# Expert weights copied and split in place, sixteen tile buffers, and the routed tiles of the last groups issued behind the shared part

## What is computed

```python
x = x + attn(layernorm(x), Wq, Wk, Wv, Wr)                  # self-attention, 16 heads of 64, causal
x = x + xattn(layernorm(x), ctx, ctx, w_q, w_k, w_v, w_o)   # cross-attention, 16 heads
x = x + ffn(layernorm(x), ...)

# ffn, flat = the 2048 tokens
shared = swiglu(flat @ w_in.T) @ w_out.T
g_probs = softmax(flat @ wg.T + gb)            # 2 groups
g_idx = argmax(g_probs)
masked = where(g_idx == group of expert, flat @ we.T + eb, -inf)
p_expert = softmax(masked) * g_probs[g_idx]    # 8 experts, 4 a group
topv, topi = top_k(p_expert, 2)                # always two experts of the chosen group
h = swiglu(flat @ w1.T)                        # 512 wide, the same for every expert
routed = sum over the two experts: (h * weight) @ w2[e].T
out = x + shared + routed
```

## Time and profile before

| | us |
|---|---|
| median of the three runs | 945.33 |
| the profiled execution | 941.11 |
| span of the profile, first to last instruction | 939.3 |
| attention, to the barrier | 0 to 649.6 |
| feed-forward, to the first slot scatter | 649.6 to 726.3 |
| scatters and what PE does beside them, to the first `turn` | 726.3 to 790.4 |
| 39 expert tiles | 790.4 to 870.3 |
| last shared units, gathers, output | 870.3 to 939.3 |

### The profile page before, as it was taken

One profiled execution on the slowest core, in us unless ns is written; L12 is line 12 of the kernel. 1 busy time (PEld: TensorE's weight loads), 2 busy tenths in 40 slices (PEclk: granted clock), 3 DMA queues, 4 the chain that ended last, 5 costly groups with the idle time before them and its releaser, 6 DMA issues. The chain is left out here.

```text
span 939.3 us, 17987 instructions
## 1 busy us (share of the span) xinstructions
PE 851.3 (91%) x6115; PEld 741.0 (79%) x6115; DVE 596.2 (63%) x1513; ACT 546.3 (58%) x1667; POOL 304.0 (32%) x318
## 2 busy tenths in 40 slices
PE   8999999999999989999999999998787748999841
PEld 6788888888888878988988898896575637999731
DVE  5787787687778767667767766775768214333153
ACT  4877677677668776866677686775343113554110
POOL 1443124124123434421432341351333750000544
PEclk9999999999999999999999999999897969999976
DMA  7680000000001020000000020010120532664233
GB/s 240 245 312 2 1 0 0 0 0 0 0 1 46 24 68 1 1 23 1 0 22 0 0 80 9 1 46 1 67 68 23 206 152 95 205 199 149 79 90 112
DMA packets 34105, 60.35 MB, mean 64 GB/s; under 512 B 3460, under 2 KB 15108, under 8 KB 34052
## 3 DMA queue, kind: packets, MB, share of 16 engines
q1 hardware_dynamic: 29956, 47.07, 15.0%
q0 software_dynamic: 4096, 12.59, 4.0%
HBM read 33.83 MB, written 25.82 MB: 64 GB/s over the span
## 5 line engine op out<-in xcount | busy, mean ns | idle before, releaser
L420 POOL TENSOR_TENSOR prob<-prob,rsum 128x512 f32<-128x512 f32 x128 | 133.4, 1042 | 395.0 <-DVE rsum L613 395.0
L498 ACT ACTIVATE prob<-psS,nmin 128x128 f32<-128x128 f32 x512 | 181.4, 378 | 6.2 <-DVE nmin L597 3.6
L481 ACT ACTIVATE pT_hi<-psT 128x512 fp32r<-128x512 f32 x128 | 69.6, 595 | 85.6 <-PE psT L752 85.6
L498 ACT ACTIVATION_READ_ACCUMULATOR prob<-psS,nmin 128x1 f32 x512 | 111.9, 218 | 0.0
L582 DVE TENSOR_TENSOR oT_lo<-psT,oT_hi 64x512 fp32r<-64x512 f32 x128 | 88.1, 688 | 23.1 <-ACT oT_hi L486 21.1
L576 DVE TENSOR_TENSOR pT_lo<-psT,pT_hi 128x512 fp32r<-128x512 f32 x128 | 82.3, 685 | 1.6 <-ACT pT_hi L481 1.4
L486 ACT ACTIVATE oT_hi<-psT 64x512 fp32r<-64x512 f32 x128 | 76.1, 594 | 5.6 <-PE psT L143 3.9
L476 ACT ACTIVATE v_hi<-psW 128x512 fp32r<-128x512 f32 x64 | 38.3, 598 | 68.0 <-PE psW L143 68.0
L141 PE MATMUL psT<-pT_lo,v_hi 128*128 128x256 f32 x256 | 73.1, 285 | 4.6 <-DVE pT_lo L576 4.6
L570 DVE TENSOR_TENSOR v_lo<-psW,v_hi 128x512 fp32r<-128x512 f32 x64 | 44.2, 691 | 50.3 <-ACT v_hi L476 50.3
L1022 POOL DMA_INDIRECT stage<-ys,slot x32 | 32.6, 1017 | 128.1 <-DMA ys<-z 99.7
(11 more groups left out here) (252 smaller groups left out, 2501.4 us busy)
## 6 DMA issues: line engine op xcount, KB each, us to landing
hs<-zero SPq DMA_DIRECT2D x1, 9984.0 KB, 31.2
stage<-hs SPq DMA_DIRECT2D x39, 256.0 KB, 2.9
stage<-w SPq DMA_DIRECT2D x10, 512.0 KB, 3.4
ys<-z SPq DMA_DIRECT2D x39, 128.0 KB, 1.9
stage<-ctxT SPq DMA_DIRECT2D x4, 512.0 KB, 4.0
out<-xres SPq DMA_DIRECT2D x16, 128.0 KB
xres<-x SPq DMA_DIRECT2D x3, 512.0 KB, 7.6
stage<-wq SPq DMA_DIRECT2D x2, 512.0 KB, 3.9
```

What stands on the lines that cost most here:

```text
L420: nc.gpsimd.tensor_tensor(prob[:, r, :], prob[:, r, :], rsum[:, r].unsqueeze(2).broadcast_to([P, TPG, P]), ALU.mult).then_inc(prob_done, 1)
L481: nc.scalar.activation(pT[0][:, i, :], psT[:, i, :], ACT.Copy).then_inc(pT_hi, 1)
L498: e = nc.scalar.activation(prob[:, n, :], flat(psS[:])[:, n * P:(n + 1) * P], ACT.Exp, bias=nmin[:, n:n + 1], scale=-1.0, accum_out=psums[ ...
```

## The change

1. **win** becomes a piece of the first block: ACT makes its `hi` and DVE its `lo` while PE ends the attention; the table of silu is loaded there too.
2. **w2**: SP copies it within DRAM (`w2_raw`, 4.19 MB, one DMA) behind the zeroing of `hs`. At the start of the second block four DMAs of 1 MB load it into the `lo` tile itself; ACT makes `hi` from there in eight parts (`w2_hi_part`) and DVE subtracts in place (`w2_lo_part`). POOL has no weights in the second block.
3. **Buffers**: 16, one for each routed tile: twelve in `stage` (in another order), two in `z`, and `above` and `ties`, which shrink from 128x768 to 128x512. No tile waits for a scatter.
4. **Gate**: ranks are compared within each group of four experts, 32 comparisons a token and not 64. One instruction makes `sel`; `unsel` and the selected `wse` are made once for all tiles by `unselected`, behind the second round. `unit(8)` stands between `gate_maxima(0)` and `gate_ranks(0)`, and ACT's `bias(3)` ahead of `exps(0)`.
5. **Order**: behind `slot_counts` PE runs S10 to S13, S20, `shared_out(1)`, and H9 to H15 last. ACT and DVE follow, with w2 parts between.

```diff
-        PIECES += ["win", "wout"] + [f"w2 {k} {half}" for k in range(HT) for half in ("lower", "upper")]
+        PIECES += ["win", "wout"]
-        H_AT = (6, 7, 10, 11, 2, 3, 4, 5, 8, 9, 0, 1)
+        H_AT = (6, 7, 8, 9, 10, 11, 0, 1, 2, 3, 4, 5)
...
                 sp.dma_start(hs.rearrange("(t p) d -> p t d", p=P),
                              zero[:].unsqueeze(1).broadcast_to([P, NT, HID])).then_inc(slots_zero, 16)
+                sp.dma_start(w2_raw, w2.rearrange("(k p) n -> k p n", p=P)).then_inc(w2_copied, 16)
...
+                act.preload_act_table(ACT.Silu)
                 pT_split(STEPS)
+                act.wait_ge(qk_mm, 2 * STEPS)
+                weights_hi(act, N_ATT + 2, wq_hi[:])
                 oT_split(STEPS, 1)
...
                 pT_split(STEPS)
+                weights_lo(dve, N_ATT + 2, wq_lo[:], wq_hi[:])
                 oT_split(STEPS, 1)
...
+            def h_slot(T):
+                if T < HSLOTS:
+                    return chunk(H_AT[T])
+                if T < HSLOTS + 2:
+                    return flat(z[:, 2 * (T - HSLOTS):2 * (T - HSLOTS) + 2, :])
+                return (above, ties)[T - HSLOTS - 2][:]
...
-            UNITS = ["H0", "H1", "H2", "H3", "S00", "S01", "S02", "S03", "H4", "H5", "H6", "H7", "H8", "H9", "H10", "H11",
-                     "H12", "H13", "H14", "H15", "S10", "S11", "S12", "S13", "S20", "S21", "S22", "S23",
+            UNITS = ["H0", "H1", "H2", "H3", "S00", "S01", "S02", "S03", "H4", "H5", "H6", "H7", "H8", "S10", "S11", "S12",
+                     "S13", "S20", "H9", "H10", "H11", "H12", "H13", "H14", "H15", "S21", "S22", "S23",
...
+                sp.wait_ge(w2_copied, 16)
+                for k in range(HT):
+                    sp.dma_start(w2s[1][:, k, :].bitcast(F32), w2_raw[k]).then_inc(w2_in[k], 16)
+
+                sp.wait_ge(scattered, B * CHOICES * 16)
...
-                late_lo(LATE.index("win"))
                 ln_scale(pool, L0 + 2)
-                late_lo(LATE.index("w2 0 lower"))
-                late_lo(LATE.index("w2 0 upper"))
                 ln_scale(pool, L0 + 3)
-                for k in range(1, HT):
...
+                def w2_hi_part(i):
+                    k, c = W2_PARTS[i]
+                    act.wait_ge(w2_in[k], 16)
+                    nc.scalar.activation(w2s[0][:, k, c], w2s[1][:, k, c].bitcast(F32), ACT.Copy).then_inc(w2_hi, 1)
...
+                def w2_lo_part(i):
+                    k, c = W2_PARTS[i]
+                    dve.wait_ge(w2_hi, i + 1)
+                    nc.vector.tensor_tensor(w2s[1][:, k, c], w2s[1][:, k, c].bitcast(F32), w2s[0][:, k, c].bitcast(F32),
+                                            ALU.subtract).then_inc(w2_lo, 1)
...
+                def unselected():
+                    dve.wait_ge(sel_done, 2)
+                    nc.vector.tensor_scalar(unsel[:], sel[:].bitcast(F32), -BIG, BIG, ALU.mult,
+                                            ALU.add).then_inc(unsel_done, 1)
+                    nc.vector.tensor_tensor(wse[:], wse[:], sel[:].bitcast(F32), ALU.mult).then_inc(unsel_done, 1)
...
                 slot_counts()
-                for T in range(9, B):
-                    unit(f"H{T}")
                 for m in range(HT):
                     unit(f"S1{m}")
                 unit("S20")
                 shared_out(1)
+                for T in range(9, B):
+                    unit(f"H{T}")
...
-                for name in LATE[2:]:
-                    wait_lo(pe, name)
+                pe.wait_ge(w2_lo, len(W2_PARTS))
```

More of the change, by code:

```diff
@@ L342, in build @@
             pieces += [(k_rows(w1)[:, :, c], w1s[0][:, :, c], w1s[1][:, :, c], 1.0) for c in (lower, upper)]
-            late_sources = [k_rows(win), k_rows(wout)] + [w2_rows[k][c] for k in range(HT) for c in range(2)]
+            pieces += [(k_rows(win), wq_hi[:], wq_lo[:], 1.0)]
+            late_sources = [k_rows(wout)]
             SWAPS = {(0, 0): ("wq upper", "wr lower"), (0, 1): ("wk upper",), (0, 2): ("wr upper",),
@@ L348, in build @@
                      (NGRP, 2): ("xr upper",), (2 * NGRP - 1, 3): ("w1 lower",), (2 * NGRP - 1, 5): ("w1 upper",)}
[L349 removed]
+            assert len(pieces) == PIECES.index("wout")
             STEPS = 2 * NGRP * PAIRS
@@ L394, in _ @@
                     load(sp, n, pieces[n][0])
-                for i in range(STAGES):
-                    load(sp, len(pieces) + i, late_sources[i])
+                load(sp, len(pieces), late_sources[0])
                 sp.wait_ge(slots_zero, 16)
@@ L1062, in _ @@
                 unit(1)
-                late_hi(0)
+                weights_hi(act, N0, late[0][1])
                 unit(2)
@@ L1099, in _ @@
                 split("S20")
+                w2_hi_part(6)
+                for u in range(UNITS.index("H9"), UNITS.index("S21")):
+                    unit(u)
+                    if u == UNITS.index("H9"):
+                        w2_hi_part(7)
                 def expert_hi(i):
@@ L1316, in _ @@
                 gate_maxima(0)
+                unit(8)
                 gate_ranks(0)
@@ L1330, in _ @@
                 slot_weights()
-                for u in range(14, UNITS.index("S10") + 1):
-                    unit(u)
-                for m in range(HT):
-                    unit(UNITS.index(f"S1{m}") + 1)
-                    split(f"S1{m}")
+                unit(14)
                 def add_shared(g):
@@ L1341, in add_shared @@
                         nc.vector.tensor_tensor(half, psA[:, i, :], half, ALU.add).then_inc(shared_added, 1)
+                for m in range(HT):
+                    u = UNITS.index(f"S1{m}") + 1
+                    if u > 14:
+                        unit(u)
+                    split(f"S1{m}")
+                    w2_lo_part(m)
                 add_shared(0)
@@ L1345, in _ @@
                 split("S20")
+                for u in range(UNITS.index("H9"), UNITS.index("S21")):
+                    unit(u)
+                    if u < UNITS.index("H9") + 4:
+                        w2_lo_part(4 + u - UNITS.index("H9"))
                 for i in range(NT):
```

132 lines of the change are left out of this document (52 added, 80 removed).

## The result

| | before | after |
|---|---|---|
| median, us | 945.36 | 908.40 |
| runs | 943.61 to 945.77 | 907.72 to 910.11 |
| the profiled execution | 941.11 | 910.11 |

The ratio is 0.9615, 95% interval 0.9596 to 0.9634.

The account below looks back on a forecast made before the run. The stretch from first scatter to first turn was taken as a chain with no engine full. 939.3 - 34.1 + 4.5 + 5.0 = 914.7 span, 916.5 in all; the same 24.6 off 945.33 gave 920.7 us, range 909 to 934.

Parts of the forecast that it names:

- From 790.4 to the end the work and its order stay: From the old first turn to the end: no change in the work or its order.
- step 3: PE's lowered clock after waits: 2.0 at shared_out(1), 2.5 for the first expert tiles, 4.5 us given back; bounds 0 and 8.
- Step 1: Up to the first scatter: shorter PE waits save 7.1, 3.7, 5.8 and 1.9, sum 18.5 us; first scatter at 707.8.
- Rival (e): PE, not DVE, was late for the gates, so the saving before the first scatter halves: 930 us; chance 0.06.
- Step 2: First scatter to first turn: PE's chain sets the first turn at 756.3, before 790.4; 34.1 less, 18.5 from before the scatters.
- Step 4: PE's completions seen late beside dense scatters: one hold of 5.0 us taken; bounds 0 and 19.5 twice.
- the same 24.6 off 945.33: Last step: the gain against the profiled execution taken off the median of the runs, giving 920.7 us.
- Experts and end as before: Listed among the expected signs: the expert tiles and the end of the kernel stay as they were.
- Step 5: The copy of w2 lies beside attention and costs nothing; 1.5 us if it held back an instruction load.
- (b): Several long holds of PE's completions beside scatters; one of 19.5 instead of 5.0 gives 935.2, within 928 to 943; chance 0.14.
- (c): Slower: each of the seven routed units behind the shared part is held 5.0, 35 against 29.6 gained: 950.7; chance 0.04.
- (d): w2 parts on DVE block POOL's scatters; four behind cost 4.9 more, less the slack: 924 to 926; chance 0.04.

Follow-up runs that it names:

- gate_wide: The changed kernel with part 4 alone undone (64 comparisons a token, old order around the gate): 909.4 us, ratio 0.964.
- pool_pieces: The changed kernel with eight idle subtractions on POOL in the place and size of the old weight pieces: 918.8 us, ratio 0.9741.
- preload: The changed kernel with the 39 loads of expert offsets into PE's registers moved out of the expert tiles to earlier places: 908.2 us, ratio 0.9602.
- twice: The changed kernel with every load of an expert's offset into PE's registers made twice: 930.5 us.
- no_copy: The changed kernel without the copy of w2 in DRAM, its four loads reading the input itself: 908.4 us, ratio 0.9621.
- gap_early: The changed kernel with all w2 lo parts behind H9 to H15, plus a POOL wait ahead of H4's scatters until S13 is split: 909.4 us, ratio 0.9606.
- twelve: The changed kernel with part 3 alone undone: twelve buffers, H12 to H15 reusing those of H0 to H3: 906.8 us, ratio 0.9587.
- order_old: The changed kernel with part 5 alone undone: H9 to H15 ahead of S10 to S13, S20 and shared_out(1): 912.7 us, ratio 0.9663.
- tail: The changed kernel with DVE adding routed rows of tiles 0 to 7 between S22 and S33, add_shared(2) behind S31: 899.7 us, ratio 0.9518.

## Why the prediction was wrong by its size

The time came 12.3 under the forecast. By the two means the gain is 36.2 where the sum had 24.6: 11.6 more. The step that failed most is "From 790.4 to the end the work and its order stay", to which step 3 added 2.5: that stage became 2.3 shorter, 4.8 of the 11.6 (item 5). The middle is 4.3 of it (items 3 and 4), the head 1.7 (item 1).

1. **Step 1, to the first scatter: right.** 18.5 forecast, 20.2 measured; 707.8 forecast, 708.3 in the first profile. The wait before H7 is gone, a comparison of 384 columns takes the 0.56 forecast, the rows 1.40. Its inner division was less right: the gate's smaller work alone is worth 0.9 once POOL is quiet (`gate_wide`), and idle pieces on POOL cost 10.6 (`pool_pieces`, which waits longer at `z_turn(3)` than the old kernel did). The rest, 8.7, with win's rows in it, no run divides. Rival (e) is out.
2. **Step 2: right up to the addition.** `add_shared(0)` done at 723.1 forecast, 723.5 measured. Then PE came late: `shared_out(1)` at 0.66 of the clock ended at 732.1, not 728.5 (730.5 with step 3's 2.0), and from H9 on POOL and not PE was the chain: 14 scatters from 737.9. In the first profile the first turn was at 761.3, the sum with its two allowances had 763.3.
3. **Step 3, the clock: near in sum (4.1 for 4.5).** `shared_out(1)` took 8.5. Its 48 matmuls need 6.0 at full clock and not the 5.4 of step 2, as the kernel before shows:

```profile
784.58:790.57 5.99, 5.99 (x50) 5.99 (x51) 0.00 (x0) 0.00 (x0) 0.00 (x0) 1.00 0.00 0
```

So the wait cost 2.5 in clock where 2.0 was allowed, and 0.6 is a term of step 2 that was too small. The first tiles lost 1.6 (6.14 to the first result, 4.53 before; 1.3 in the second profiles), not 2.5, and 0.63 of the 1.6 is a wait for the second load.

4. **Step 4, late completions: the mechanism was right, the amounts were not.** I allowed 5.0 for one hold. One of 2.2 came, and it cost the chain only 0.9. From the end of `shared_out(1)` to the end of the last scatter the first profile took 24.7, where the sum had 27.9 with its hold. Behind the scatters it took 0.4 less, and `shared_out(1)` 1.1 more (item 3): the middle is 2.5 under the 55.5 forecast. The other part is in the kernel before, whose holds I had read from one execution; with its second profile the mean middle is 1.9 longer. So the last step, "the same 24.6 off 945.33", failed too: it took the 4.2 us between profile and median for something that the change leaves alone, and about half of what divides the two old profiles stands in the middle, where the change acts.
5. **"Experts and end as before": wrong, 4.8 of the miss.** Forecast 2.5 slower, measured 2.3 faster (2.0 and 2.6 in the two pairs of profiles). 2.1 to 2.4 is the sequencer's lead (`preload`, `twice`), of which I had read nothing since the rows count PE as busy. 1.5 is a stretch of lowered clock in `shared_out(2)`: 7.5 us in both old profiles, 6.0 in both new ones; 31 matmuls before, 42 after, in like windows:

```profile
885.00:890.00 5.00, 5.00 (x31) 5.00 (x30) 0.00 (x0) 0.00 (x0) 2.73 (x3) 0.66 0.37 105
```

```profile
855.40:860.40 5.00, 5.00 (x42) 4.91 (x41) 0.00 (x0) 0.00 (x0) 2.68 (x3) 1.00 0.36 105
```

What brings it isn't shown. In `no_copy` and `gap_early`, whose order is the new one, `shared_out(2)` took 7.5 again, and 6.0 in the other eight profiles with the old end. This part of the miss may be chance.

6. **Step 5, nothing for the copy: right** (`no_copy`), and nothing for the buffers either (`twelve`), of which the sum had no term.
7. **Rivals.** (b) and (c) did not come. (c)'s mechanism is real in another order: in `order_old` it took four shared units. (d)'s mechanism is real too, and cheap. A scatter that starts while DVE subtracts a w2 part is held nearly until the subtraction ends: with 0.80 us of the part left it took 0.66 longer than its 0.97, with 0.38 left 0.25, with 0.37 left 0.23, with 0.33 left 0.20. In `preload` 1.11 left made 0.98 more. A scatter that starts 0.4 before a part takes its 0.97. Over the 14 scatters this makes 1.3, not 4.9, since each waits only for the rest of a part. By the Trainium skill, SBUF — State Buffer, "Who interferes with whom", a DVE instruction with two SBUF inputs contends with a GpSimd one that reads SBUF, and the page infers that the making of descriptors is left alone. The trace agrees with the first (a scatter reads its slots from SBUF) and doesn't bear out that a scatter as a whole is left alone. The earlier trace rows couldn't show it, since the old kernel has no weight subtraction beside a scatter. The longest in the changed kernel:

```profile
738.99 1.22 DVE L1235 TENSOR_TENSOR w_lo<-w_lo,w_hi 128x1024 fp32r<-128x1024 f32 x1
...
739.41 1.63 POOL L1000 DMA_INDIRECT hs<-stage,slot  x1 [0.30 <-DVE stage L1224]
```

Against the two means: 1.7 (step 1) + 4.3 (middle) + 4.8 (end) + 0.2 = 11.0 of the 11.6 between 24.6 and 36.2; the rest lies outside the spans.

## What to carry to other kernels

Take the difference between two executions of the kernel before as a part of its profile: if a wait has no visible cause (a bank read microseconds after its last matmul), it can vary, and a change that removes it can gain more than one profile shows. Don't place anything that waits for PE's completion beside a dense run of indirect DMAs if it can stand before or behind it. An engine shown as busy can still be paced by its instruction stream: compare the count of instructions in equal windows, and look where register loads stand.

## What the runs showed that I had not expected

- Completions of PE are seen late beside dense runs of POOL's indirect DMAs (one in 1.28 us), by up to 26 us. The first late one came 10 to 24 us into a run (7.9 behind `gap_early`'s pause), but not every run has one: H9 to H15 of the changed kernel ended up to 13.5 us into the second run, and none was late. None came at one DMA in 2.3 us or more with a small instruction between. Beside gathers too: `shared_out(3)` was 5.0 to 6.2 late in all fourteen profiles with the old end.
- Held completions come out in their order, 0.12 to 0.13 us apart: S31 and S32 of `tail` at 870.44 and 870.57, H15 and S10 of the kernel before at 768.72 and 768.84. What frees them is open: often it is about 2 us behind the run's end, but in `gap_early` and the earlier trace rows within the run.
- A register load that the array's work seemed to hide costs 0.13 us a tile (74.9 less 69.7 over 39), a second one 0.57 (95.1 less 72.8).
- An instruction of DVE that issues 0.12 us ahead of a long one on POOL can take as long as that one (4.76), and one that issues 0.25 ahead 0.40, while a product (0.69) and the four statistics (1.40) beside the same piece took what they always take.
